# A convolution with a quantised MLP and a routed expert layer: weight steps of the opening reordered, first input pair split, no GpSimd drain at the block's end

## The reference

```python
x = x + L0_ffn(L0_cond(x, cond, conv weight, cond weight, channel bias), NF4 codes and scales, LoRA tables, biases)
x = x + L1_ffn(L1_cond(x, cond, perceptron and 8 kernels), gate, 8 experts)

# L0_cond: grouped 9-tap convolution along 1024, 32 batches x 64 channels, plus cond @ weight.T + bias
# L0_ffn:
vals  = NF4[codes] * repeat(absmax, 64)          # up: 2752 x 1024, down: 1024 x 2752
y1    = x1 @ w_up + b_up + x1 @ a_up @ b_up_lora
y2    = relu(y1) @ w_down + b_down + relu(y1) @ a_dn @ b_dn
# L1_cond: softmax(perceptron(cond)) mixes 8 kernels of 64 x 64, one per batch; applied over the channels
# L1_ffn: each of 2048 rows goes to the expert of its largest gate logit: x @ expert_w[j].T + expert_b[j]
```

## Time and profile before

| what | value |
|---|---|
| median of 3 runs | 1428.24 us (1428.13 to 1430.22) |
| profiled execution | 1424.34 us |
| its span, first to last instruction | 1422.7 us |
| mean granted TensorE clock | 0.993 |
| busy: PE, DVE, ACT, POOL | 1385.2, 1136.3, 754.9, 213.2 us |

### The profile page before, as it was taken

How to read it: one execution, slowest core, us unless ns; L and a number is a source line. 1 busy time by engine, 2 the same in 40 slices (tenths; PEclk the granted TensorE clock), 3 DMA queues, 4 the chain that set the end, 5 groups by cost and what they waited for, 6 DMA issues and landing times.

```text
span 1422.7 us, 20751 instructions
## 1 busy us (share of the span) xinstructions
PE 1385.2 (97%) x6881; PEld 1141.3 (80%) x6881; DVE 1136.3 (80%) x1119; ACT 754.9 (53%) x839; POOL 213.2 (15%) x234
## 2 busy tenths in 40 slices
PE   7899999999999999999999999999999999999996
PEld 7887888888888888888888888888766788788884
DVE  5868887878878788787887878877655799899994
ACT  5656555454554545545455454553204377677772
POOL 0111000000000000000000000000014266564462
PEclk9999999999999999999999999999999999999998
DMA  6864567477774777747676476765858746979951
GB/s 204 328 236 154 203 233 266 169 286 227 255 261 174 285 222 257 258 176 285 220 260 256 177 285 219 261 254 170 293 190 296 277 119 168 336 229 304 344 154 30
DMA packets 102938, 331.51 MB, mean 233 GB/s; under 512 B 15476, under 2 KB 23164, under 8 KB 102876
## 3 DMA queue, kind: packets, MB, share of 16 engines
q1 hardware_dynamic: 79556, 258.56, 49.0%
q0 software_dynamic: 23072, 71.85, 18.0%
q10 hardware_dynamic: 256, 0.40, 0.1%
HBM read 295.63 MB, written 46.14 MB: 240 GB/s over the span
## 4 chain that ended last, share of the span: by engine, by line
PE 91%; DVE 3%; DMA 2%; issue 1%; ACT 1%; ACTq 0%; SPq 0%; DVEq 0%; POOL 0%; POOLq 0%
PE pair L1140 27%; PE pair L1141 26%; PE pair L1142 26%; PE pair L1194 4%; PE pair L1416 1%; PE pair L1342 1%; PE pair L1333 1%; DVE wf L810 1%; DMA wraw<-exp_w 1%; PE pair L1221 1%; PE pair L1278 1%; PE pair L1204 1%; PE pair L1351 1%; PE pair L1383 1%; DVE wlr L1115 1%
## 5 line engine op out<-in xcount | busy, mean ns | idle before, releaser
L810 DVE TENSOR_TENSOR wf<-wf,term 128x1024 f32<-128x1024 f32 x308 | 376.7, 1223 | 65.8 <-ACT term L599 50.7
L599 ACT ACTIVATE term<-codes 128x1024 f32<-128x1024 int32 x308 | 320.6, 1054 | 139.4 <-DVE wf L810 139.4
L1140 PE MATMUL pair<-wh,hh 128*128 128x512 f32 x672 | 263.4, 392 | 3.2 <-DVE ring L873 1.4
L1141 PE MATMUL pair<-wl,hh 128*128 128x512 f32 x672 | 262.0, 390 | 0.0
L1142 PE MATMUL pair<-wh,hl 128*128 128x512 f32 x672 | 262.0, 390 | 0.0
L1140 PE MATMUL pair<-ring,wh 128*128 128x512 f32 x656 | 255.6, 390 | 0.0
L1141 PE MATMUL pair<-ring,wh 128*128 128x512 f32 x656 | 255.3, 389 | 0.0
L1142 PE MATMUL pair<-ring,wl 128*128 128x512 f32 x656 | 255.2, 389 | 0.0
L743 ACT ACTIVATE whr<-wraw 128x1024 fp32r x184 | 188.1, 1056 | 84.3 <-PE pair L1142 48.2
L868 DVE TENSOR_TENSOR acc<-acc,pair 128x1024 f32<-128x1024 f32 x160 | 194.4, 1217 | 47.1 <-PE pair L1142 39.8
L1115 DVE TENSOR_TENSOR wlr<-wraw,whr 128x1024 fp32r<-128x1024 f32 x184 | 213.2, 1220 | 7.8 <-ACT whr L743 7.5
(11 more groups left out here) (180 smaller groups left out, 1510.5 us busy)
## 6 DMA issues: line engine op xcount, KB each, us to landing
ring<-x_parts SPq DMA_DIRECT2D x320, 512.0 KB, 6.5
wraw<-exp_w SPq DMA_DIRECT2D x64, 512.0 KB, 12.1
x_parts<-stage POOLq DMA_DIRECT2D x24, 512.0 KB, 6.5
xg<-exp_b POOLq DMA_DIRECT2D x23, 512.0 KB, 7.9
codes<-codes_up SPq DMA_DIRECT2D x22, 512.0 KB, 6.1
codes<-codes_dn SPq DMA_DIRECT2D x22, 512.0 KB, 5.7
am<-am_dn SPq DMA_DIRECT2D x22, 512.0 KB, 3.9
acc<-x_nat POOLq DMA_DIRECT2D x16, 512.0 KB, 5.4
```

The lines of the kernel that those rows point to most:

```text
L599: return nc.scalar.activation(out, codes[:, n % 2], ACT.Relu, scale=scale, bias=-scale * bend)
L810: nc.vector.tensor_tensor(whole(n), whole(n), term[:, e % 2], op).then_inc(term_added, 1)
L1140: mm(ps, ah, bh, start=first, stop=False)
L1141: mm(ps, ah, bl, start=False, stop=False)
```

## The change

Three edits. First, the block is opened without a drain for GpSimd. Second, SP loads the first input pair in two transfers, the first on a new semaphore that conv(0) waits for, the second behind the first codes; conv(1) waits for it. Third, the weight steps of the opening are in another order in the lists of ACT and DVE, and the two LoRA products inside the convolution move from behind conv(6) and conv(15) to behind conv(5) and conv(13).

```diff
+        first_in = sem("first_in")
-        block = ctx.enter_context(nc.Block())
+        block = ctx.enter_context(nc.Block(no_gpsimd_drain=True))
...
-            load_pair(0)
+            sp.dma_start(xcv0[:, 0], x_conv[:, 0]).then_inc(first_in, 16)
             load_codes(0, 0)
+            sp.dma_start(xcv0[:, 1], x_conv[:, 1]).then_inc(xcv_in[0], 16)
             load_pair(1)
...
+            head(0, 0)
+            ramps(0, 0, (1, 2))
             for k in range(FIRST):
                 conv_high(k)
-                if k == 0:
-                    head(0, 0)
-                if k < 3:
-                    ramps(0, 0, (k + 1,))
-                elif k == 3:
+                if k < 2:
+                    ramps(0, 0, (k + 3,))
+                elif k == 2:
                     act.wait_ge(ffn_const, 32)
                     nc.scalar.activation(lora[:], lora_f[:], ACT.Copy).then_inc(lora_split, 1)
                     lora_high(0, 0)
-                elif k < 8:
-                    ramps(0, 0, (k,))
-                elif k == 8:
-                    head(0, 1)
-                elif k == 9:
-                    ramps(0, 1, (1,))
-                elif k == 10:
+                elif k < 6:
+                    ramps(0, 0, (k + 2,))
+                elif k == 6:
+                    head(0, 1)
+                elif k == 7:
+                    ramps(0, 1, (1,))
+                elif k == 8:
                     high(0, 0)
                     lora_high(0, 1)
-                elif k < 17:
-                    ramps(0, 1, (k - 9,))
-                elif k == 17:
-                    head(0, 2)
-                elif k == 18:
-                    ramps(0, 2, (1,))
-                elif k == 20:
+                    ramps(0, 1, (2,))
+                elif k < 14:
+                    ramps(0, 1, (k - 6,))
+                elif k == 14:
+                    head(0, 2)
+                elif k == 15:
+                    ramps(0, 2, (1,))
+                elif k == 17:
                     high(0, 1)
+                elif k in (18, 19):
+                    ramps(0, 2, (k - 16,))
             lora_high(0, 2)
-            ramps(0, 2, range(2, 8))
+            ramps(0, 2, range(4, 8))
             high(0, 2)
             relu(0, 0)
...
+            add_ramps(0, 0, (1,))
             for k in range(FIRST):
                 conv_low(k)
                 if k < 3:
-                    add_ramps(0, 0, (k + 1,))
+                    add_ramps(0, 0, (k + 2,))
                 elif k == 3:
...
                     lora_low(0, 0)
-                elif k < 8:
-                    add_ramps(0, 0, (k,))
-                elif k == 8:
-                    scale(0, 0)
-                elif k == 9:
-                    add_lora(0, 0)
-                elif k == 10:
-                    add_ramps(0, 1, (1,))
-                elif k == 11:
+                    add_ramps(0, 0, (5,))
+                elif k < 6:
+                    add_ramps(0, 0, (k + 2,))
+                elif k == 6:
+                    scale(0, 0)
+                elif k == 7:
+                    add_lora(0, 0)
+                elif k == 8:
+                    add_ramps(0, 1, (1,))
+                elif k == 9:
                     low(0, 0)
                     lora_low(0, 1)
-                elif k < 18:
-                    add_ramps(0, 1, (k - 10,))
-                elif k == 18:
-                    scale(0, 1)
-                elif k == 19:
-                    add_lora(0, 1)
+                    add_ramps(0, 1, (2,))
+                elif k < 15:
+                    add_ramps(0, 1, (k - 7,))
+                elif k == 15:
+                    scale(0, 1)
+                elif k == 16:
+                    add_lora(0, 1)
+                elif k == 17:
+                    add_ramps(0, 2, (1,))
+                elif k == 18:
+                    low(0, 1)
                 else:
-                    add_ramps(0, 2, (1,))
-            low(0, 1)
+                    add_ramps(0, 2, (k - 17,))
             lora_low(0, 2)
-            add_ramps(0, 2, range(2, 8))
+            add_ramps(0, 2, range(4, 8))
...
-                if k % 2 == 0:
+                if k == 0:
+                    pe.wait_ge(first_in, 16)
+                elif k == 1 or k % 2 == 0:
                     pe.wait_ge(xcv_in[p % 4], 16 * (p // 4 + 1))
...
-                if k == 6:
+                if k == 5:
                     pe.wait_ge(lora_split, 2)
                     lora_product(0, 0)
-                elif k == 15:
+                elif k == 13:
                     lora_product(0, 1)
```

## The result

| what | before | after |
|---|---|---|
| median | 1428.18 us, 4 runs (1427.2 to 1430.22) | 1412.17 us, 4 runs (1408.62 to 1414.68) |
| ratio | 1 | 0.9889 [0.9866, 0.9913] |
| profiled execution, span | 1424.34, 1422.7 us | 1414.34, 1412.4 us |
| mean granted clock | 0.993 | 0.998 |

The change saves 16.0 us by the medians. The profiled pair differs by 10.0 only; where its other 6 us went is read last. The new lines push numbers on: L1140 is now L1151, L1142 L1153, L1190 L1203, L1194 L1207, L634 L636, L628 L630, L845 L850, L743 L748, L1115 L1126.

What follows compares the result with a forecast made beforehand. TensorE was taken as 91% of the chain, so its start, seam and clock counted, plus GpSimd's drain as path at the end. 7.1 + 8.97 = 16.1 us off the median 1428.24 gives 1412.1; range 1410.7 to 1418.1, holding 0.80.

Steps and rivals of the forecast that it cites:

- 7.1: Opening, up to the first up product: first pair, gap and clock together, 0.71 + 3.92 + 2.50 us saved.
- No drain, 8.97 us: Block's end: GpSimd's DRAIN falls away, out_done still waits for the last scatter; 8.97 us saved, bounds 0 and 9.2.
- The gap, 3.92 us: Between conv(20) and the first up product: low(0,1) comes sooner, so up(0,0) starts at 55.56 instead of 59.48.
- The clock, 2.50 us: First up product: with no gap the clock stays at 2.4 GHz, 11.53 us instead of 14.03; bounds 0 and 3.0.
- The first pair, 0.71 us: Start: half the bytes land sooner, so conv(0) starts 0.71 us sooner, at 8.64; bounds 0 and 1.42.
- The lower bound on the start: Start of conv(0): the toeplitz table lands at 7.89 us and becomes the bound, which limits the gain to 1.42 us.
- 0.36: At conv(0): if the clock's rise stays at its moment, half of the 0.71 us is lost; 0.71 was kept.
- The tie behind it: Behind the first up product: PE releases relu(0,0) at 66.67 us, ACT's high(0,2) lets it issue at 66.71; loss counted 0.
- The median, 3.9 us over the profiled execution: Whole kernel: timed median 1428.24 us against 1424.34 profiled, accounted for by no row; 16.1 was taken from the median.
- the forecast span, 1406.6: Whole kernel: the profiled span after the change, forecast near 1406.6 us against 1422.7 before.
- Rival E's point of decision: Opening: slower because ACT waits for codes ahead of conv_high(0); PE pays from codes at 14.6 us; chance 0.03.
- the cover of lora_product(0, 0): Behind conv(5): lora_low(0,0) ends by 22.3, product from about 22.9, 0.6 us spare; without it PE pays at most 1.22.

Runs made afterwards that it cites:

- e1: The kernel before with only the block opened without the GpSimd drain; 1418.52 us, ratio 0.9929.
- e2: The changed kernel with the drain put back, so split first pair and new order of weight steps alone; 1418.22 us, ratio 0.9937.
- e10: The changed kernel run once more, unchanged; 1411.81 us, ratio 0.9872 against the kernel before.
- e8: The kernel before with the waits for the last scatters moved from POOL to SP, so POOL drains while the last is under way; 1425.16 us.
- e4: The kernel before with the new order of weight steps alone, drain kept; 1422.38 us.
- e9: The changed kernel with the first codes issued behind input pairs 1 and 2 and lora_product(0, 0) back behind conv(6); 1411.76 us.
- e3: The kernel before with the first input pair in two transfers alone, drain kept; 1423.15 us.
- e5: The kernel before with fourteen dummy matmuls of 512 columns in PE's gap before the first up product; 1426.04 us.
- e6: The changed kernel with eleven dummy matmuls ahead of conv(0), the first at 1.84 us; 1410.33 us, ratio 0.9874 against the kernel before.
- e11: The same kernel as e6, eleven dummy matmuls ahead of conv(0), measured again; 1409.16 us, ratio 0.9870 against the kernel before.
- e7: The changed kernel with the first codes issued behind input pairs 1 and 2, so that they land later; 1415.53 us.

## Why the prediction was right

1412.1 us was forecast and 1412.17 measured, in the range, and by the mechanism forecast: the two halves alone, e1 and e2, save 8.8 and 9.1 us where 8.97 and 7.1 were counted, each inside its interval. That forecast and median agree to 0.1 us is luck: the ratio's interval leaves 12.4 to 19.1 us for the gain, and the same kernel measured again (e10) gains 17.1 by the medians. In the traces the opening is worth 6.6 us rather than 7.1: relu(0,0) starts at 73.27 on average in before, e1 and e8, and at 66.63 in after, e2 and e10.

- **No drain, 8.97 us.** Right; 0.3 of it comes back outside the span (1.64 us there before, 1.94 after). The Trainium skill (VectorE: DVE Perf Modes, "The DRAIN you can't avoid") tells of short constant DRAINs of about 12 ns on all engines before and behind the kernel. The one here lasts 8974 ns, and it does not come back behind the block: the time outside the span grew by 0.3 us only.
- **The gap, 3.92 us.** Right to the hundredth, and no luck: up(0,0) follows conv(20) by 1.70 or 1.71 us in after, e2, e4, e9 and e10, and by 5.62 or 5.63 in before, e1, e3 and e8. low(0,1) ran from 52.14 to 53.36, where 53.6 was forecast as its end.
- **The clock, 2.50 us.** Right here (2.52), and e5 shows the cause. As a constant it was too firm: with the same gap, relu(0,0) starts 14.32, 14.64, 13.44 and 13.45 us behind up(0,0) in before, e1, e3 and e8, and 11.95 in after: 1.5 to 2.7 us. The lower clock's stretch is not of one length.
- **The first pair, 0.71 us: mis-sized at the start of conv(0).** The trace of before had the latest landing. The whole pair lands 6.6, 5.9, 6.1, 5.8 and 6.0 us behind its issue (before, e1, e4, e5, e8; mean 6.1), the half with the codes right behind it 5.7, 4.8, 5.9, 5.0, 5.8 and 5.2 (after, e2, e3, e6, e10, e11; mean 5.4): the 0.7 is there on average. The start of conv(0) gets less of it: 9.35, 8.65, 8.87, 8.56 and 8.78 with the whole pair (mean 8.84), 8.48, 8.34, 8.65 and 8.57 with the half (after, e2, e3, e10; mean 8.51), so 0.3 us. The lower bound on the start that was named, the table's landing, is not what binds: in e2 the half had landed at 7.5 and the matmul waited for the context product on DVE (L799), a term that the sum does not have. Whether the rise of the clock moves with the start, the question behind 0.36, stays open: the moment differs from trace to trace of one kernel, conv(1)'s sixteen matmuls lasting 1.95 us in after and 2.54 in e10. The Trainium skill (TensorE: Matmul & The Clock Gate, Part 1) says that the gate's window does not start anew with the kernel; moments that differ in one kernel agree with that.
- **The tie behind it.** ACT's high(0,2) and relu were forecast to tie with PE at 66.7 us. They do, at 66.61; ACT has no idle time before relu, so any further gain on PE needs ACT's and DVE's chain to follow, as it did in e11 by 2.3 us.
- **The median, 3.9 us over the profiled execution.** It was carried along unexplained. The traces differ most in the expert stage (270.4 to 277.3 us), and before's trace had the shortest one of all thirteen. After's is 5.3 us longer, most of the 5.8 by which the forecast span, 1406.6, was missed. That the medians' 3.9 us lie in the same stage is likely but not shown, since the other runs have no trace; that the median came out right while the span did not owes something to that.
- **Rival E's point of decision: wrong.** It was put at codes landing at 14.6 us, by way of conv(4). e7 shows that the cover of lora_product(0, 0), stated as 0.6 us and 0.9 in after (lora_low ends at 21.73, the product starts at 22.61), is used up first. Codes 2.8 us late cost 2.6 us at relu(0,0), although conv(0) started 0.4 sooner: 1.52 is the wait, and 1.3 more is the lower clock in the sixteen matmuls behind it (3.24 against 1.95).

## What to carry to other kernels

When the last thing on the path is a block's own DRAIN, see what it waits for: here it was a fixed 9 us of one engine after every result had landed, and the explicit wait on the results, which the kernel had already, was enough without it. An idle stretch on TensorE can cost the clock on top of its own length (3.68 and 1.52 us did here, 0.48 us in e5 did not); remove it by taking the work that nobody needs yet out from in front of the step that is waited for. A single trace sets the size of a transfer's landing badly: take such a term from several.

## What was not expected of the hardware

GpSimd's DRAIN lasts 8974 ns to the nanosecond in before, e2, e3, e4 and e5, where it starts between 1407.7 and 1415.2 us, and in e8 its 9 us begin when the last scatter's instruction is over, ahead of its landing. TensorE with work almost without a break from 1.84 us ran conv(0) at half rate in one trace and at full rate in another, so here work ahead of the first convolution did not buy the upper clock for certain. An idle time of 1.52 us was enough to lose it in e7 for about 3 us; the same seam of 3.68 us was followed by 5.2 us at granted clock 0.50 in before and in e1, and by a mean of 0.67 over that stretch in e3.
